# Reciprocal roots of the query and key norms: from one three-step Newton iteration per pair of tiles on GpSimd to one per tile, begun on ScalarE

## The reference

```python
def l2norm(t):
    return t / jnp.maximum(jnp.linalg.norm(t, axis=-1, keepdims=True), 1e-12)
...
        q = l2norm(q) * qs
        k = l2norm(k) * ksc
...
        q = q * cos * scale + rotate_half(q) * sin * scale
        inv = 1.0 / scale
        k = k * cos * inv + rotate_half(k) * sin * inv
        out = local_attention(q, k, v)
...
    for i in range(DEPTH):
        x = attn_layer(shift_tokens(x), Wqkv[i], q_scale[i], k_scale[i], Wo[i]) + x
        x = ffn_layer(shift_tokens(x), ln_g[i], ln_b[i], W1[i], b1[i], W2[i], b2[i]) + x
```

## Time and profile before

| | us |
|---|---|
| median of 3 runs | 2068.67 (2067.4 to 2084.68) |
| profiled execution, device time | 2063.68 |
| its span in the trace | 2061.9 |
| PE busy | 1876.6 |
| DVE busy | 1657.8 |
| POOL busy | 1464.0 |
| ACT busy | 1307.4 |

### The profile page before, as it was taken

One profiled execution on the slowest core, in us unless ns is written; L12 is line 12 of the kernel. 1 busy time (PEld: TensorE's weight loads), 2 busy tenths in 40 slices (PEclk: granted clock), 3 DMA queues, 4 the chain that ended last, 5 costly groups with the idle time before them and its releaser, 6 DMA issues.

```text
span 2061.9 us, 74558 instructions
## 1 busy us (share of the span) xinstructions
PE 1876.6 (91%) x32776; PEld 1256.8 (61%) x32776; DVE 1657.8 (80%) x1819; ACT 1307.4 (63%) x1723; POOL 1464.0 (71%) x1467
## 2 busy tenths in 40 slices
PE   3999997689999999999999998999999999999985
PEld 1434443366676666666667666766666666766764
DVE  5777770688898898889888898889888988888852
ACT  1356566556766776677667765776677667766652
POOL 1011112999988889888988797889888978898910
PEclk7699999799999999999999999999999999999997
DMA  3141100132333333333233323233332333222221
GB/s 103 33 144 51 46 25 22 39 85 70 76 89 76 86 77 82 91 77 88 66 76 80 98 64 89 66 87 86 76 88 71 82 89 76 68 70 65 70 64 47
DMA packets 144035, 151.51 MB, mean 73 GB/s; under 512 B 60760, under 2 KB 85596, under 8 KB 142944
## 3 DMA queue, kind: packets, MB, share of 16 engines
q1 hardware_dynamic: 143712, 146.75, 28.3%
HBM read 35.75 MB, written 5.44 MB: 20 GB/s over the span
## 4 chain that ended last, share of the span: by engine, by line
PE 32%; POOL 23%; DVE 23%; issue 14%; ACT 3%; SPq 3%; DMA 1%; POOLq 0%; DVEq 0%; ACTq 0%
POOL arena L1138 9%; POOL arena L1146 6%; DVE ss L731 4%; PE banks L484 4%; DVE arena L642 3%; PE banks L421 3%; PE banks L578 3%; PE banks L493 3%; DVE mx_t L766 3%; DVE arena L739 3%; PE banks L511 3%; PE banks L524 2%; DVE arena L780 2%; PE banks L561 2%; SPq L1302 2%
## 5 line engine op out<-in xcount | busy, mean ns | idle before, releaser
L1138 POOL TENSOR_TENSOR arena<-arena,tab_sl 128x512 f32<-128x512 f32 x384 | 593.6, 1575 | 15.0 <-ACT arena L938 8.3
L1146 POOL TENSOR_TENSOR arena<-arena 128x1024 f32<-128x1024 f32 x192 | 490.3, 2575 | 0.0
L739 DVE TENSOR_TENSOR arena<-arena,rn 128x1024 f32<-128x1024 f32 x192 | 364.4, 1939 | 109.4 <-POOL rn L1114 109.4
L484 PE MATMUL banks<-w_qkv,arena 128*128 128x512 f32 x768 | 360.9, 614 | 17.4 <-ACT arena L930 10.7
L967 ACT ACTIVATE arena<-arena 128x1024 f32<-128x1024 f32 x96 | 101.5, 1057 | 407.3 <-DVE arena L770 407.3
L484 PEld LDWEIGHTS banks<-w_qkv,arena 128*128 128x128 f32 x768 | 140.9, 193 | 170.1 <-issue 161.5
L642 DVE TENSOR_REDUCE arena<-banks 128x1 f32<-128x512 f32 (+3 forms) x352 | 183.5, 587 | 67.6 <-PE banks L381 58.4
L493 PE MATMUL banks<-ident,arena 128*128 128x128 f32 x1536 | 202.8, 285 | 38.0 <-DVE arena L780 21.6
L780 DVE TENSOR_TENSOR arena<-banks,tab_cl 128x1024 f32<-128x1024 f32 x192 | 226.2, 1219 | 12.7 <-ACT arena L938 11.2
L1080 POOL TENSOR_SCALAR_AFFINE_SELECT arena<-arena 128x512 f32<-128x512 f32 x64 | 40.9, 640 | 269.0 <-ACT arena L888 268.8
L561 PEld LDWEIGHTS banks<-w_o,arena 128*128 128x128 f32 x1536 | 187.7, 194 | 57.4 <-issue 33.0
(11 more groups left out here) (108 smaller groups left out, 3000.7 us busy)
## 6 DMA issues: line engine op xcount, KB each, us to landing
arena<-arena SPq DMA_DIRECT2D x1512, 64.0 KB
arena<-parts_dram SPq DMA_DIRECT2D x64, 144.0 KB
w_qkv<-Wqkv SPq DMA_DIRECT2D x6, 1024.0 KB
parts_dram<-arena SPq DMA_DIRECT2D x12, 256.0 KB, 3.0
tab_cl<-tab_c SPq DMA_DIRECT2D x6, 512.0 KB, 7.4
tab_sl<-tab_s SPq DMA_DIRECT2D x6, 512.0 KB
w_o<-Wo SPq DMA_DIRECT2D x6, 512.0 KB
w_qkv<-Wqkv SPq DMA_DIRECT2D x6, 512.0 KB, 4.3
```

The source lines that it names most:

```text
L484: last = e.matmul(ps[:, BANK * c:BANK * (c + 1)], xsT[b][:, P * t:P * (t + 1)], w_qkv[:, at:at + BANK], start=True, stop=True)
L739: e.tensor_tensor(to, to, rn[n // 2 % 2][:, n % 2, HEADS * m:HEADS * (m + 1)].unsqueeze(2).to_broadcast([P, HEADS, HEAD_DIM]), ALU.mult).t ...
L1138: e.tensor_tensor(qk_sw[:, m, :].rearrange("p (h d) -> p h d", d=HEAD_DIM)[:, :, d:d + HALF], raw[:, m, :].rearrange("p (h d) -> p h d", d ...
L1146: e.tensor_tensor(to, to, qk_sw[:, m, :], ALU.add).then_inc(S["rs"], 1)
```

## The change

The roots are made tile by tile. `ss` and `rn` become four buffers of one tile each. ACT gets a function `roots(j)`, called in `project(n)` for tile n - 1 between the copies and the Squares, with three instructions of 128x32: Relu(ss - 1e-24), Ln(that + 1e-24), Exp(-0.5 times that). POOL's `norms(j)` is called in each step for one tile: it floors `ss` and multiplies it by -0.5 in one instruction, then makes one Newton step of four instructions. Both bounds, -1e-24 and 1e-24, lie in a small tile `floor`. ACT is told to load one table set, which holds Exp and Ln, at the start and again behind each gelu. DVE's `norms` and `scale` only change buffers and the counts that they wait for.

```diff
-        rs_g, minus_half = sb("rs_g", [P, 2 * RS]), sb("minus_half", [P, tiles])
+        rs_g, minus_half = sb("rs_g", [P, RS]), sb("minus_half", [P, tiles])
+        floor = sb("floor", [P, 2])
...
-        ss, rn = [[sb(f"{name}{i}", [P, 2, RS]) for i in range(2)] for name in ("ss", "rn")]
+        ss, rn = [[sb(f"{name}{i}", [P, RS]) for i in range(4)] for name in ("ss", "rn")]
...
             def norms(n):
                 w.wait_ge(S["sq"], 2 * n + 2)
-                w.wait_ge(S["rn"], n // 2 - 1 if n >= 2 else 0)
+                w.wait_ge(S["rn"], max(0, n - 3))
...
             def scale(n):
-                w.wait_ge(S["rn"], n // 2 + 1)
+                w.wait_ge(S["rn"], n + 1)
...
+            def roots(j):
+                y, v = rn[j % 4][:, :], ss[j % 4][:, :]
+                w.wait_ge(S["ss_sum"], j + 1)
+                w.wait_ge(S["rot"], max(0, 2 * (j - 3)))
+                w.wait_ge(S["floor"], 2)
+                e.activation(y, v, ACT.Relu, bias=floor[:, 0:1]).then_inc(S["root"], 1)
+                w.wait_ge(S["root"], 3 * j + 1)
+                e.activation(y, y, ACT.Ln, bias=floor[:, 1:2]).then_inc(S["root"], 1)
+                w.wait_ge(S["root"], 3 * j + 2)
+                e.activation(y, y, ACT.Exp, scale=-0.5).then_inc(S["root"], 1)
...
                 w.wait_ge(S["ss_sum"], n)
+                if n:
+                    roots(n - 1)
                 for m in range(2):
...
                 if ff_here and k == 3:
                     ff_gelu(G)
+                    e.preload_act_table_set(ACT_SET)
...
             def norms(j):
-                y, v = (t[j % 2].rearrange("p i h -> p (i h)") for t in (rn, ss))
+                y, v = rn[j % 4][:, :], ss[j % 4][:, :]
                 t = rs_g[:, :]
-                w.wait_ge(S["ss_sum"], 2 * j + 2)
-                w.wait_ge(S["rot"], max(0, 4 * (j - 1)))
-                e.tensor_scalar(v, v, NORM_FLOOR ** 2, None, ALU.max).then_inc(S["newton"], newton.up())
+                w.wait_ge(S["root"], 3 * j + 1)
+                e.tensor_scalar(v, v, NORM_FLOOR ** 2, -0.5, ALU.max, ALU.mult).then_inc(S["newton"], newton.up())
+                w.wait_ge(S["root"], 3 * (j + 1))
+                e.tensor_tensor(t, y, y, ALU.mult).then_inc(S["newton"], newton.up())
                 w.wait_ge(S["newton"], newton.n)
-                e.tensor_scalar(y.bitcast(I32), v.bitcast(I32), -0.5, RSQRT_MAGIC, ALU.mult, ALU.add
-                                ).then_inc(S["newton"], newton.up())
-                for i in range(3):
...
-                last.then_inc(S["rn"], 1)
+                e.tensor_tensor(t, t, v, ALU.mult).then_inc(S["newton"], newton.up())
+                w.wait_ge(S["newton"], newton.n)
+                e.tensor_scalar(t, t, 1.5, None, ALU.add).then_inc(S["newton"], newton.up())
+                w.wait_ge(S["newton"], newton.n)
+                e.tensor_tensor(y, y, t, ALU.mult).then_inc(S["rn"], 1)
...
-                if 0 <= s - 1 < n_tiles and s % 2 == 0:
-                    norms((s - 2) // 2)
+                if 0 <= s - 1 < n_tiles:
+                    norms(s - 1)
```

23 lines of the change are left out of this document (9 added, 14 removed).

## The result

The changed kernel takes 2052.26 us (median of 7 runs, 2049.53 to 2060.46). The kernel before, run more often by then, has a median of 2074.14 us (7 runs, 2067.4 to 2084.68), so the ratio is 0.9908 [0.9881, 0.9934]: 0.9% faster. The forecast was 1.9%, 2030 us against 2068.67. The direction was right and the time lies in the range, but half of the gain is missing. The question of the experiments is where that half went.

What follows compares the result with a forecast made beforehand. PE was taken to bound the kernel, DVE second, POOL pacing the start. Gains of 18.5 us at the start, 18 steady and 2 at the end, 38.5 off 2063.7, gave 2025, as a median 2030 us; 8-in-10 range 1996 to 2066.

Steps and rivals of the forecast that it cites:

- the wait for `rn`: DVE's scale (L739) waiting for POOL's reciprocal roots: 109.4 us in 48 waits, to fall under 15 us.
- the first scale: At the start, DVE's first scale was to begin at about 375.4 us instead of 387.94.
- the first 11.5 us: Start: 12.5 us from the earlier first scale, 11.5 left after ACT's three instructions ahead of the first scores.
- the other 7 us of the start: Start, before 600 us: 7 us gained out of 17.0 us of DVE's further waits, since PE is close behind.
- So ACT: 0: ACT's three instructions, some 1.05 us a tile, were to cost no time; bounds 0 and 18 us lost.
- The bound of 18: Upper loss on ACT: 0.25 us in 72 tiles if the turned-query copy's 1.3 us cover falls short.
- 48 us of new collisions: DVE's scale coming into POOL's running rotate: 1.0 us more for each of 48 even tiles.
- at most 58.4 us can be had there: Steady part, 601 to 1897 us: 1296 us less PE's 1237.6 busy caps any gain.
- PE's limit: Rival: all steady PE idle time goes, 92 us gained in all, median 1977 us; chance 0.12.
- slower by SBUF: Rival: scale falls on POOL's rotate adds, 2.15 us for each of 48 even tiles; median 2082 us; chance 0.06.
- Eaten on ACT: Rival: start gain comes, steady gives nothing, ACT's three cost 18 us; some 2068 us; chance 0.19.
- The sign that I named: PE's waits for ACT's copies (L956, L930) growing by more than 10 us would show the forecast wrong.

Runs made afterwards that it cites:

- The pairs with one Newton step: Kernel before, still in pairs and without ACT's three instructions, with one Newton step instead of three: 0.9899, 2061.56 us.
- the second execution: Changed kernel, unchanged, profiled once more beside later runs on the same chip: 0.9903 to the kernel before, 2051.0 us.
- the two kernels of the sections on the gelu values and the transfers: Changed kernel with the third gelu in its own buffer: 0.9907; changed kernel with one of three row copies per group made by POOL: 0.9895, 2045.42 us.
- the roots last: Changed kernel with ACT's Relu, Ln and Exp behind everything else in every ACT step: 0.9821 to the kernel before, 2032.6 us.
- the toll doubled in the other steps: Changed kernel with a second Relu, Ln and Exp on a spare tile in all steps but the gelu steps: 0.9991 to the kernel before.
- the fastest kernel: Changed kernel with ACT's three last in every step, the third gelu's own buffer and POOL's copy of rows: 0.9772, 2022.13 us.

## Why the prediction was right in sign and wrong in size

**Right: the wait for `rn` and what it hides.** It fell to 5.0 us (forecast: under 15), and waits for PE took its place as expected. The pairs with one Newton step show that such waits are far from worth their face, 79 us of them for 1% of the time, with scale longer at the same time.

**Right: the first scale; nearly right: the first 11.5 us.** Counted from the first raw copy the first scale was forecast at 15.4 us and came at 15.0. The first maximum gained 9.6 us instead of 11.5, for the 4.12 us that the second scale waits for POOL. By the raw copy of tile 5 the gain is 13.4.

**Wrong: the other 7 us of the start.** They were to come out of the six waits behind the first, 17.0 us up to 600. Instead 4 to 7 us of the 13.4 are given back between tiles 5 and 16: 8.0 us are left at tile 16 on the means, against 18.5. The trace shows two places. The first is a stand of PE that the kernel before doesn't have: ACT waits for rows that SP's transfers bring, and PE for ACT's copy behind that.

```profile
514.00 1.01 ACT L978 COPY arena<-banks 128x1024 f32<-128x1024 f32 x1 [5.92 <-DMA arena<-arena]
...
517.15 6.18 PE L485 MATMUL banks<-w_qkv,arena 128*128 128x512 f32 x8 [6.03 <-ACT arena L932]
```

In the second execution PE stands for 6.31 us there. The pairs with one Newton step, without ACT's three, have it too (5.90), so it does not need the three. The second place is in the middle of PE's scores, at 415.7 to 422.0: 6.36 us with no releaser named, 6.86 in the second execution, and 2.63 and 4.15 us in the two of the kernel before. Why it grew stays open. The toll of the next point does not show in the start: up to tile 16 it takes 233.1 us with ACT's three out, and 233.0 and 232.9 in the two kernels of the sections on the gelu values and the transfers, which keep them. With the roots last it is 228.5; 3.5 of these 6 us less are the first stand (2.57).

**Wrong, and the main miss: "So ACT: 0".** The price of the three was right: 0.88 us a tile against 1.05. The Trainium skill, page "ScalarE: Activation LUTs", section "What ACT_TABLE_LOAD costs", from which the prediction had an estimate of 0.3 + 0.3 + 0.2 = 0.8 us, agrees with the rows (0.329, 0.322, 0.230). The failing step is the one that asked where they are covered. The forecast looked at ACT's copy of the turned queries (L956, 1.3 us of cover), which does hold at 0.88 us, and went on to say that on the gelu step DVE's 2.18 us wait for PE takes them in. It never laid the copy of the gathered values (L977) beside L524, which needs the banks that it leaves. That hand-over has 1.1 us of cover in some gelu steps and 0.2 to 0.3 us in the others, and the copy moved from 0.15 us behind the start of PE's transposes (L568) to 0.93 behind it (L569), from one frequent value to the other. Taking the three out is worth 12 to 20 us and moving them to the end of the step 18 us. Some 8 to 10 us are seen at this hand-over; where the rest is paid stays open, and a part of it may be TensorE's clock, as the windows of the kernel with the roots last show. The bound of 18 was about the size, but hung on an instruction that still had its cover. The kernel with the toll doubled in the other steps shows that one giving way, with 8.6 us, only at twice the load.

The sum with this one term put right is 18.5 to 26.5 us (38.5 less 20 or 12), against 21.9 by the medians. That closeness is partly luck, since 10 us of the start are missing too; the steady part brought 8.7 us on the means with the toll in it, so 21 to 29 without, where 18 were counted. Its own uncertainty is as large.

**Not shown: 48 us of new collisions.** The mean of scale went from 1939 to 1991 ns, 10 us over 192 instructions instead of 48. The forecast named the phase of scale against rotate as a risk. The runs show how strong it is: the median of scale is 2127 ns before, 2119 after, and 1214 with the roots last. That it was not on the path is likely but not shown: the kernel without ACT's three gains its 1% with scale as long as ever, and the kernel with the roots last, where scale is short, gains no more, but there the product L760 got longer.

**Wrong: "at most 58.4 us can be had there".** I took PE's busy time in the steady window as fixed (1237.6 us of 1296). The same kernel has 1246.7 in its second execution. In the fastest kernel it is 1219.8 us for the same 76 tiles, 18 less, at a granted clock of 1.00 instead of 0.99, that is at 2.4 GHz throughout instead of with six short stretches at 1.2. The projection's matmuls take 627 ns on the mean in the changed kernel and 611 with the roots last. So the window less the busy time is no upper bound of a gain.

**The rivals.** PE's limit (0.12) and slower by SBUF (0.06) did not come. "Eaten on ACT" (0.19) had the mechanism right, ACT's three against too small a cover, but its 18 us were set against a steady gain of nothing; the two pairs of profiles show a steady gain of about 9 us net of the toll, and the time lies between it and the forecast. The sign that I named, PE's waits for ACT grown by over 10 us, did come: from 340 to 2062 us PE waits 24.7 us for the copies of the shifted rows where it was 10.7 (22.0 where it was 14.4 in the second executions). But it is a sign of something else. With ACT's three out the same wait is 24.8 us, and 6.0 of the changed kernel's are the stand in the start. The toll itself shows in this list only as the 4.5 us of L525 in the steady window (first line: the shifted rows there; the kernel without the three has 16.1 us at the first and none at the second):

```profile
PE banks L485 <- ACT arena L932: 12.9, 7, 5.6
...
PE banks L525 <- ACT arena L992: 4.5, 12, 0.4
```

The stretch around L525 is 8 to 10 us longer in sum than without the three. Half of that appears as later starts with no wait on record. The third rival's price was also half of its own mechanism: 2.15 us for each even tile is one instruction of scale, and a tile has two. Scale rose by 10 us in all, so nothing hung on it.

## What to carry to other kernels

When small work is put into the middle of an in-order engine's step, list every reader of what that engine does behind it, in each kind of step (here one in four has one more user of the PSUM banks), and compare the smallest cover with the new work; an average of 31% idle says nothing. If nobody needs the small work's result soon, put it last in the step: the same three instructions cost 12 to 20 us in the middle and nothing that could be measured at the end. Look at the cover in every instance of a step, not in one: here it was 1.1 us in some and 0.3 in others. And profile both kernels twice before reading a 10 us difference between stretches, and read the granted clock beside them; two executions of one kernel differed by 12 us, 9 of them in PE's busy time.

## What was not expected of the hardware

What an elementwise instruction on DVE takes goes with what POOL does beside it. In the kernel with the roots last POOL does nothing beside 55 of the 192 instructions of scale, and these take 1.20 to 1.23 us; the others take from 1.21 up to 3.39. The excess can move from one instruction to another when small work elsewhere is moved: scale 1.21 or 2.12 us at the median, the first part of POOL's rotate 1.13 or 1.57 us on the mean, the product L760 1.46 or 2.04 us, in kernels that do the same work.

One product L759 took 8.70 us, once in fourteen traces; no other DVE product took more than 3.49. Beside it POOL ran five instructions of its rotate, one behind the other, and it ended 1.09 us behind the last of them (1275.03 us):

```profile
1266.13 4.31 POOL L1138 TENSOR_TENSOR arena<-arena,tab_sl 128x512 f32<-128x512 f32 x4
1267.42 8.70 DVE L759 TENSOR_TENSOR arena<-arena,rs_o 128x1024 f32<-128x1024 f32 x1
1270.40 4.63 POOL L1146 TENSOR_TENSOR arena<-arena 128x1024 f32<-128x1024 f32 x2
```

The Trainium skill, page "SBUF — State Buffer", section "Who interferes with whom", says that whichever of the two engines issues first gets the port pair that they share for the whole instruction, and that the other fully blocks. If the other is then served next, a wait is one POOL instruction long at most, here some 2.4 us. The rows up to 3.49 agree with that; the row of 8.70 does not.

POOL's one-operand instruction on 32 elements took 0.41 us on the mean where the like one on 64 elements took 0.26. With the roots last, the same instruction took 0.30 (L1125 there). So its length does not follow its size alone. That what runs beside it decides would fit, but was not looked at by itself.
